# Expert stages by pairs of quads: one relu to a pair, eight second products in a row

## The reference

```python
def _L0_ffn_ref(x, controller, f1, f2):          # after a layernorm
    t = NEXPERTS                                  # 16 rows make a group
    grouped = x.reshape(B, S // t, t, D)
    cont_logits = jnp.einsum('bgtd,des->bgtes', grouped, controller) + tie
    cont_perm = (cont_logits == jnp.max(cont_logits, axis=-3, keepdims=True)).astype(x.dtype)
    intermediate = jnp.einsum('bgtd,desf->bgtesf', grouped, f1)
    inner = jax.nn.relu(jnp.einsum('bgtesf,bgtes->bgesf', intermediate, cont_perm))
    inter2 = jnp.einsum('bgesf,esfd->bgesd', inner, f2)
    return jnp.einsum('bgesd,bgtes->bgtd', inter2, cont_perm)
```

## Time and profile before

| | |
|---|---|
| median of 3 runs | 769.68 us (769.06 to 771.16) |
| span of the profiled execution | 768.9 us |
| PE busy | 714.7 us (93%) |
| DVE busy | 584.6 us (76%) |
| ACT busy | 545.0 us (71%) |
| POOL busy | 181.3 us (24%) |
| moves, scratch<-stage | 64, 512 KB each, 4.3 us from issue to landing |
| gathers, stage<-scratch | 96, 256 KB each, 4.4 us |

### The profile page before, as it was taken

One profiled execution on the slowest core, in us unless ns is written; L12 is line 12 of the kernel. 1 busy time (PEld: TensorE's weight loads), 2 busy tenths in 40 slices (PEclk: granted clock), 3 DMA queues, 4 the chain that ended last, 5 costly groups with the idle time before them and its releaser, 6 DMA issues.

```text
span 768.9 us, 22658 instructions
## 1 busy us (share of the span) xinstructions
PE 714.7 (93%) x7206; PEld 554.5 (72%) x7206; DVE 584.6 (76%) x2402; ACT 545.0 (71%) x1622; POOL 181.3 (24%) x375
## 2 busy tenths in 40 slices
PE   7899999999999999999999999868998988987945
PEld 7788888888888888888888888646555555554623
DVE  6789899898898898898988988847656656654612
ACT  4889899989998898999899988835454454452510
POOL 2030230330321312303303213537225225200000
PEclk9999999999999999999999999999999999998969
DMA  6876876786787777867867776840699999999999
GB/s 181 196 172 163 187 189 159 170 193 155 171 192 168 165 185 169 187 164 167 195 148 177 173 163 134 220 139 2 270 325 304 382 314 307 370 316 305 377 355 326
DMA packets 121494, 166.01 MB, mean 216 GB/s; under 512 B 15296, under 2 KB 84416, under 8 KB 121184
## 3 DMA queue, kind: packets, MB, share of 16 engines
q1 hardware_dynamic: 118944, 163.18, 76.7%
q10 hardware_dynamic: 2304, 1.58, 0.8%
q0 software_dynamic: 192, 0.52, 0.2%
HBM read 47.78 MB, written 41.94 MB: 117 GB/s over the span
## 4 chain that ended last, share of the span: by engine, by line
PE 79%; DMA 9%; DVE 4%; SPq 3%; issue 2%; ACT 2%; POOL 0%; DVEq 0%
PE bank L636 14%; PE bank L588 14%; PE bank L623 8%; PE bank L660 8%; PE bank L649 8%; PE bank L610 7%; PE bank L812 6%; DMA stage<-scratch 5%; PE bank L791 5%; PE bank L780 3%; DMA scratch<-stage 2%; PE bank L838 2%; SPq L399 2%; PE bank L581 2%; DMA XRlast<-scratch 1%
## 5 line engine op out<-in xcount | busy, mean ns | idle before, releaser
L956 ACT ACTIVATE Ps<-Ps,nmax 128x256 f32<-128x256 f32 x512 | 254.6, 501 | 19.9 <-DVE nmax L1170 19.7
L1170 DVE CUSTOM_DVE_ANT_0 Ps<-bank,masks 128x256 f32<-128x256 f32 x512 | 192.7, 420 | 27.3 <-issue 27.3
L636 PE MATMUL bank<-ident,Ps 128*128 128x128 f32 x1024 | 134.7, 274 | 2.0 <-ACT Ps L956 1.3
L636 PEld LDWEIGHTS bank<-ident,Ps 128*128 128x128 f32 x1024 | 114.7, 141 | 11.5 <-issue 3.4
L588 PE MATMUL bank<-hT,WT 128*128 128x256 f32 x512 | 121.1, 380 | 0.5 <-ACT hT L913 0.4
L588 PEld LDWEIGHTS bank<-hT,WT 128*128 128x128 f32 x512 | 92.4, 190 | 11.0 <-ACT Vs L929 0.8
L513 POOL TENSOR_SCALAR h<-X,mv,roots 128x256 f32<-128x256 f32 x64 | 79.3, 1252 | 87.8 <-PE bank L780 82.4
L956 ACT ACTIVATION_READ_ACCUMULATOR Ps<-Ps,nmax 128x1 f32 x512 | 97.7, 191 | 0.0
L623 PE MATMUL bank<-stack 128*128 128x256 f32 x512 | 91.4, 311 | 0.8 <-DMA stack<-parts 0.8
L1181 DVE COPY PTs<-bank 128x512 f32<-128x512 f32 x128 | 86.4, 675 | 0.2
L623 PEld LDWEIGHTS bank<-stack 128*128 128x128 f32 x512 | 71.5, 189 | 17.9 <-issue 13.1
(11 more groups left out here) (100 smaller groups left out, 1051.4 us busy)
## 6 DMA issues: line engine op xcount, KB each, us to landing
stack<-parts SPq DMA_DIRECT2D x506, 128.0 KB, 2.5
scratch<-stage SPq DMA_DIRECT2D x64, 512.0 KB, 4.3
stage<-scratch SPq DMA_DIRECT2D x96, 256.0 KB, 4.4
X<-in_x SPq DMA_DIRECT2D x32, 256.0 KB, 2.9
rbc<-turned SPq DMA_DIRECT2D x128, 64.0 KB, 2.1
out<-X SPq DMA_DIRECT2D x32, 256.0 KB, 4.3
XRlast<-scratch SPq DMA_DIRECT2D x16, 512.0 KB, 8.7
f1s<-in_L_ffn_f SPq DMA_DIRECT2D x1, 2048.0 KB, 9.2
```

Of the source, the lines that this page charges most:

```text
L636: last = nc.tensor.transpose(PTb[h % 2][:, k * N + t * P:k * N + t * P + P], Ps[:, pr % 2, t, h % 2, k * P:k * P + P], ident[:, :])
L956: last = nc.scalar.activation(Ps[:, pr % 2, t, h, :], Ps[:, pr % 2, t, h, :], ACT.Exp, bias=nmax[:, pr % 2, t, h:h + 1], scale=-1.0, accum ...
L1170: last = nc.vector.tensor_tensor_reduce(out=Ps[:, pr % 2, t, h, :], in0=s_bank(n)[:, h * N:h * N + N], in1=masks[:, t, :], scale=1.0, scal ...
```

## The change

A stage goes by pairs of quads, w = 0 to 7. expand(w) makes the 16 products of two quads into the two halves (128 columns each) of bank w % 2 and raises in_ready once. One relu of 128x256 takes both to inner (ScalarE for even w, VectorE for odd w). contract(w) first waits for the relu, for ScalarE's copies of pair w - 2 and for VectorE's copies of pair w - 1, and then makes its eight products in a row: the four of the first quad into columns 0 to 255 of four banks, the four of the second into columns 256 to 511 of the same banks. f2_ready is raised once, at the end of the eight. VectorE and ScalarE then make two copies each, one to a quad, of the same size as before. SP's code is the same: still a move to a quad. TensorE runs a pair ahead where it ran a quad ahead. The waits for the chunk before (fin_done, perm_saved, perm_done) stand before the first contract instead of the second.

```diff
-        def first_bank(q, hf):
-
-            return 4 + 2 * ((2 * q + hf) % PAIRS_OF_BANKS) if (2 * q + hf) % PAIRS_OF_BANKS < 2 else 2
+        def first_bank(w, hf):
+
+            return 4 + 2 * ((2 * w + hf) % PAIRS_OF_BANKS) if (2 * w + hf) % PAIRS_OF_BANKS < 2 else 2
 
         def products(q, hf):
 
-            b = first_bank(q, hf)
-            return stage[:, q % SLOTS, 2 * hf:2 * hf + 2, :], banks[:, b:b + 2, 0:D]
+            w, i = divmod(q, 2)
+            b = first_bank(w, hf)
+            return stage[:, q % SLOTS, 2 * hf:2 * hf + 2, :], banks[:, b:b + 2, i * D:i * D + D]
...
-            def expand(c, q):
-
-                if q > 1:
-                    per, before = relu_half(q - 2)
-                    pe.wait_ge((in_act, in_dve)[q % 2], c * per + before + 1)
-                for k in range(KT):
-                    for j in range(4):
-                        last = nc.tensor.matmul(bank[q % 2][32 * j:32 * j + 32, 0:CG],
-                                                f1s[:, k, 4 * q + j, :], XS[:, k, row_of(4 * q + j), :],
-                                                start=(k == 0), stop=(k == KT - 1))
+            def expand(c, w):
+
+                if w > 1:
+                    pe.wait_ge((in_act, in_dve)[w % 2], (c * TWOS + w - 2) // 2 + 1)
+                for i in range(2):
+                    q = 2 * w + i
+                    for k in range(KT):
+                        for j in range(4):
+                            last = nc.tensor.matmul(bank[w % 2][32 * j:32 * j + 32, i * CG:i * CG + CG],
+                                                    f1s[:, k, 4 * q + j, :], XS[:, k, row_of(4 * q + j), :],
+                                                    start=(k == 0), stop=(k == KT - 1))
                 last.then_inc(in_ready, 1)
 
-            def contract(c, q):
-
-                n = c * QUADS + q
-                per, before = relu_half(q)
-                pe.wait_ge((in_act, in_dve)[q % 2], c * per + before + 1)
-                if q == 1:
+            def contract(c, w):
+
+                n = c * TWOS + w
+                pe.wait_ge((in_act, in_dve)[w % 2], n // 2 + 1)
+                if w == 0:
                     if c > 0:
                         pe.wait_ge(fin_done, c * (CT // 2))
                     following = min((c + 1) * UNITS, CHUNKS * UNITS - 1)
                     pe.wait_ge(perm_saved, following + 1)
                     pe.wait_ge(perm_done, min(following + AHEAD, CHUNKS * UNITS))
                 for hf in range(2):
-                    if 2 * q + hf >= PAIRS_OF_BANKS:
-                        pe.wait_ge((st_act, st_dve)[hf], n - 1 + hf)
-                    for j in (2 * hf, 2 * hf + 1):
+                    if 2 * w + hf >= PAIRS_OF_BANKS:
+                        pe.wait_ge((st_act, st_dve)[hf], 2 * (n - 1 + hf))
+                for i in range(2):
+                    for j in range(4):
                         r = slice(32 * j, 32 * j + 32)
-                        last = nc.tensor.matmul(bank[first_bank(q, hf) + j % 2][:, 0:D], inner[r, q % INNERS, :],
-                                                f2s[r, q, :], start=True, stop=True)
-                    last.then_inc(f2_ready, 1)
+                        last = nc.tensor.matmul(bank[first_bank(w, j // 2) + j % 2][:, i * D:i * D + D],
+                                                inner[r, 2 * (w % RELUS) + i, :], f2s[r, 2 * w + i, :],
+                                                start=True, stop=True)
+                last.then_inc(f2_ready, 1)
...
                 expand(c, 0)
-                for q in range(QUADS):
-                    if q + 1 < QUADS:
-                        expand(c, q + 1)
-                    contract(c, q)
+                for w in range(TWOS):
+                    if w + 1 < TWOS:
+                        expand(c, w + 1)
+                    contract(c, w)
...
-                def save_inner(q):
-                    act.wait_ge(in_ready, c * QUADS + q + 1)
-                    if q >= INNERS:
-                        act.wait_ge(f2_ready, (c * QUADS + q - INNERS) * 2 + 2)
-                    nc.scalar.activation(inner[:, q % INNERS, :], bank[q % 2][:, 0:CG], ACT.Relu).then_inc(in_act, 1)
+                def save_inner(w):
+                    act.wait_ge(in_ready, c * TWOS + w + 1)
+                    if w >= RELUS:
+                        act.wait_ge(f2_ready, c * TWOS + w - RELUS + 1)
+                    s = 2 * (w % RELUS)
+                    nc.scalar.activation(inner[:, s:s + 2, :].rearrange("p i g -> p (i g)"), bank[w % 2][:, 0:2 * CG], ACT.Relu)\
+                        .then_inc(in_act, 1)
                 save_inner(0)
-                for q in range(QUADS):
-                    if q + 1 < QUADS and (q + 1) % 2 == 0:
-                        save_inner(q + 1)
-                    act.wait_ge(f2_ready, (c * QUADS + q) * 2 + 2)
-                    s = q % SLOTS
-                    if landed(c, q) > 16:
-                        act.wait_ge(moved[s], landed(c, q) - 16)
-                    nc.scalar.copy(*products(q, 1)).then_inc(st_act, 1)
+                for w in range(TWOS):
+                    if w + 1 < TWOS and (w + 1) % 2 == 0:
+                        save_inner(w + 1)
+                    act.wait_ge(f2_ready, c * TWOS + w + 1)
+                    for q in (2 * w, 2 * w + 1):
+                        if landed(c, q) > 16:
+                            act.wait_ge(moved[q % SLOTS], landed(c, q) - 16)
+                        nc.scalar.copy(*products(q, 1)).then_inc(st_act, 1)
```

More of the change, by code:

```diff
@@ L43, in gnn_moe_kernel @@
     QUADS = ES // 4
+    TWOS = QUADS // 2
     SLOTS = 5
@@ L48, in gnn_moe_kernel @@
     AHEAD = 2
-    INNERS = 8
+    RELUS = 4
     PAIRS_OF_BANKS = 3
@@ L332, in landed @@
             return (c * uses_of_slot(i % SLOTS) + i // SLOTS + 1) * 16
-        def relu_half(q):
-            return QUADS // 2, q // 2
         @block.sync
@@ L1399, in experts, with save_inner @@
             def experts(c):
[L1400 to L1404, removed]
-                        .then_inc(in_dve, 1)
[L1406 to L1413, removed]
+                def save_inner(w):
+                    dve.wait_ge(in_ready, c * TWOS + w + 1)
+                    if w >= RELUS:
+                        dve.wait_ge(f2_ready, c * TWOS + w - RELUS + 1)
+                    s = 2 * (w % RELUS)
+                    nc.vector.tensor_scalar(inner[:, s:s + 2, :].rearrange("p i g -> p (i g)"), bank[w % 2][:, 0:2 * CG],
+                                            0.0, None, ALU.max)\
+                        .then_inc(in_dve, 1)
+                for w in range(TWOS):
+                    if w + 1 < TWOS and (w + 1) % 2 == 1:
+                        save_inner(w + 1)
+                    dve.wait_ge(f2_ready, c * TWOS + w + 1)
+                    for q in (2 * w, 2 * w + 1):
+                        if landed(c, q) > 16:
+                            dve.wait_ge(moved[q % SLOTS], landed(c, q) - 16)
+                        nc.vector.tensor_copy(*products(q, 0)).then_inc(st_dve, 1)
             for c in range(CHUNKS):
```

## The result

The changed kernel takes 773.95 us (median of 22 runs, 770.35 to 777.36) where the kernel before takes 770.58 in the same comparison (22 runs). The ratio is 1.0044 with an interval of 1.0028 to 1.0060: **3.4 us slower, 2.2 to 4.6**. The forecast was 771.3 in a range of 768.0 to 774.0, with the largest chance, 0.66, on no difference beyond 0.3%, and a leaning to slower, 0.28.

What follows compares the result with a forecast made beforehand. The DMA queue, not TensorE, was taken to set each stage's last landing. Later first landings of +0.4, +0.3, 0 and +0.9 us in the four chunks summed to +1.6 us on 769.68, giving 771.3 us, range 768.0 to 774.0.

Steps and rivals of the forecast that it cites:

- First move: Start of an expert stage: four quads expanded before the first contract make the first move go 1.36 us later.
- First landing: First move's landing in each stage: later by 0.4, 0.3, 0 and 0.9 us in chunks 0 to 3.
- Pace: TensorE and VectorE alternate within a stage: a pair takes 2.57 us (2.51 to 2.62), against 2.70 before.
- What is queued behind it: Stage's DMA queue, busy from second move to last: last landing is first landing plus 15 x 1.38 = 20.7 us.
- the sum of a rival: Last landing under the slower alternation: 2.8 us plus 0.7 us for the second move of a couple waiting behind the first.
- The bounds: Four stages' total: +5.4 us if the queue hid nothing; -1.2 us, or -3.0 at the far end, if never full.
- if the queue hid nothing: Upper bound over the four stages: the late first move arrives in full, 4 x 1.36 = +5.4 us.
- The queue keeps up: Rival, stage transfers: last landing follows last issue, 0.3 us earlier per chunk; 768.5 us, down to 766.7; chance 0.17.
- The slower alternation: Rival, stage pairs: 2.94 us a pair, slower from 2.76; +7.1 us, 776.8 us, or halfway 772.7; chance 0.16.
- TensorE sets the pace: Rival, expert stages: TensorE's own 2.09 us is the pair's period and transfers follow; 754.9 us; chance 0.02.
- The clock: Rival, expert stages: clock falls as TensorE waits longer; at half clock some 40 us more; chance 0.03.

Runs made afterwards that it cites:

- the second pair: The kernel before and the changed kernel, each run and profiled once more unchanged: +0.5 us (-1.4 to 2.3) and +2.5 us (0.4 to 4.7).
- fast_before: The kernel before with stage copies of half the width, but for the first five quads of chunk 0: -0.6 us (-2.2 to 1.0).
- half_after: The changed kernel with moves of half the size, partitions 0 to 63 only: +1.7 us (0.2 to 3.2) against the kernel before.
- late_before: The kernel before with six extra products that nothing reads ahead of each stage's first contract: +7.8 us (5.2 to 10.4).
- thin_before: The kernel before with moves of half the size, every second partition: -1.3 us (-2.9 to 0.3).
- fast_after: The changed kernel with stage copies of half the width, but for the first five quads of chunk 0: +4.5 us (2.0 to 6.9) against the kernel before.
- early_pairs: The changed kernel with the first and last two quads of a stage as single steps: +3.6 us (1.9 to 5.4) against the kernel before.
- thin_after: The changed kernel with moves of half the size, every second partition: +0.1 us (-1.8 to 1.9) against the kernel before.

## Why the prediction held, and which term was too small

*First move.* Forecast 1.36 us later; 3.79 to 3.82 us after the first expand against 2.48 to 2.50, so 1.31. From the contract's start to VectorE's first copy it is 1.20 to 1.22 us, where the scatter's rows gave 1.18.

*First landing.* From the first expand the sum put it at 6.6 to 6.7 us in all four chunks. Measured: 6.47, 6.67, 6.44, 6.47, which are +1.2, +0.3, -0.3 and +0.7 against before. That the stores of the chunk before hide the late start up to here in chunks 1 and 2 was right.

*Pace.* Forecast 2.57 us (2.51 to 2.62), measured 2.64. The alternation is there; the wait ahead of the contract was the small part left out, 0.14 us instead of 0.04. The last issue came 0.04 to 0.34 us later instead of 0.3 earlier.

*What is queued behind it.* **This is the step that failed.** The sum took 15 x 1.38 us from first to last landing, whatever the issue, since the moves "find it busy from the second move to the last". Measured it is 21.2, 21.9, 21.5 and 21.4 us, where 20.7 to 21 was to be seen; chunks 1 to 3 took 21.0, 20.9 and 21.0 before. So the last landing comes +0.7, +1.2, +0.2 and +1.1 us later, 3.3 in sum in this pair of profiles, instead of 1.6. Split at the first landing, the forecast was +2.6 us up to it and -1.0 behind it (chunk 0, 20.7 against 21.7 before). Measured it is +1.9 and +1.4 in this pair, +2.8 and -0.1 in the second pair, on average +2.3 and +0.7: the first landings were forecast well, and what comes behind them was 1.7 us short.

Two things were wrong there. The queue is not busy from the second move on: in chunks 0 and 3 of after the first of a couple lands in 2.65 to 2.92 us up to the fifth move, with nothing ahead of it. For most of a stage moves in a full queue land 1.21 to 1.25 us apart, between stalls of 0.7 to 1.3 us, some two or three to a stage, so that 1.38 to 1.40 is no single rate of the queue. (It isn't always 1.23 between stalls: the moves of chunk 2 of before, but for the last, land evenly 1.27 to 1.47 apart, and in chunks 1 and 2 of fast_before, with 4.9 to 6.2 us to land, many land 1.31 to 1.43 apart. No run here says why.)

The second thing is the couple: in before the last move has 1.43 us behind its neighbour and in after 0.60, and with nothing queued the second of a couple waits 0.6 to 0.8 us for the first (half_after; in chunk 0 of after 3.4 us to land against 2.7). I had this 0.7 us, but in the sum of a rival only, for a queue that has run dry. Whether it costs anything in a loaded queue isn't shown: in chunk 0 the last move lands 1.25 us behind its neighbour in both kernels. In chunks 1 and 2 of after it lands 2.27 and 2.05 us behind it, some 3 us after a load of instructions (at 624.40 and 682.46; last section), and in the second profile 2.22 and 2.53; in before only chunk 2 has this (1.75 and 2.61). How much of the loss behind the first landing is the couples, and how much is where these loads fall, stays open.

*The bounds* told the truth better than the middle. late_before shows 1.0 of 1.5 us of a late start arriving at the last landing, between the forecast and "if the queue hid nothing". fast_before shows 0.6 of 2.0 us of an early finish arriving there. So the queue swallowed most of a gain and a third of a loss. That the time still lies in the range, by 0.05 us, owes something to luck: the range reached up to 774.0 for a late start hardly hidden and for a slower alternation, and not for what was lost behind the first landing.

*The rivals.* The queue keeps up: no; the last landing came 3.0 us later in sum and the last issue 0.5. Moves that wait in line mostly landed 1.21 to 1.25 us apart, and the stage's mean of 378 GB/s holds the stalls too. The Trainium skill's ceiling of 435 GB/s ("DMA: Bandwidth & Descriptors", Specifications) gave 1.21 us to a move, by an estimate. The trace agrees with that page there, though not in the stretches at 1.31 to 1.43 us. The slower alternation: no, 2.64 is below the 2.76 from which it would have counted. TensorE sets the pace: no; its idle time in each pair stood there as forecast. The clock: granted 1.00 as long as TensorE worked in the four stages of this profile, though not in all others (last section).

*What isn't settled.* Why an earlier last landing gives back so little: thin_before lands 5.6 us earlier in sum, and the time gains 1.3 (-0.3 to 2.9). In its profile 3.4 us are gained from the first expand to the end, and the units behind the landings are 2.2 us longer (31.0 us from the last landing to the next first expand ahead of chunk 1, 29.6 before), so another wait is next there; no run here names it.

## What to carry to other kernels

Work that is made in larger steps hands over its first piece later and its last pieces together. Here a transfer queue that is nearly full stands behind it: the last piece landed later though it was issued at nearly the same time, and the 15 us that TensorE saved were worth nothing.

The spacing of landings in a profile isn't the capacity of a queue while the issues come at the same spacing; a run that issues faster tells them apart. And when two profiles are compared, count from a mark behind the last place where runs of one kernel differ among themselves.

## What the runs showed of the hardware

**The clock can fall where a stage ends.** The last contract of a stage has no expand ahead of it. In the changed order TensorE is idle for 1.49 us ahead of it; in the order before it waits 0.31 us. In the second profile of the changed kernel the granted clock fell there, in chunk 2, to 0.50 (1.2 GHz); the stretch ahead of it and the stretch itself:

```profile
664.00:678.40 14.40, 10.50 (x224) 7.67 (x220) 7.98 (x14) 6.36 (x13) 0.00 (x0) 1.00 1.01 393
678.40:681.60 3.20, 3.20 (x24) 2.22 (x22) 1.29 (x2) 1.17 (x3) 0.00 (x0) 0.50 0.88 349
```

```profile
677.87 1.69 PE L811 MATMUL bank<-f2s,h2T 32*128 32x256 f32 x16 [1.49 <-DVE stage L1417]
```

The contract took 1.69 us instead of 1.15, and the last issue came 0.5 us later. The same happened in chunk 2 of fast_after and in chunks 1 and 2 of early_pairs and thin_after, and at the end of none of the first three stages in the kernels with contracts by quads. Behind the last stage it fell in both orders (at 734.9 us in before, 738.2 in after). In the units, stretches at 0.50 come and go in either kernel: with 6.8 us of it ahead of chunk 3 the profile of after needs 29.8 us from the last landing to the next first expand, and without it the second one 27.8.

**Moves from 64 adjacent partitions follow one another nearly as slowly as moves from 128**: the couples of half_after mostly land 1.18 us apart for 256 KB, against 1.21 to 1.25 for 512 KB; only behind a late landing did they come 0.6 to 0.8 apart. From every second partition 256 KB land some 0.6 us apart.

**Late landings follow loads of instructions.** In chunk 1 of before packets of 16 KB on the queue for instructions stand at 603.51, 611.75 and 618.43, and the landings 3.1 to 3.6 us behind each come 1.9 to 2.2 us after the one before instead of 1.23. This was seen side by side, not tested; in fast_before such loads stand in chunk 3 too (717.10, 723.05, 730.56), and no landing there comes over 1.30 us after the one before.
